# dt goes into the decays' exponent, and the other chunk's values meet their probabilities in three rounded products

## The reference, cut to what matters

```python
dt = softplus(h @ Win.T + dt_bias);  g = dt * A;  G = cumsum(g) within a chunk of 128
x_c     = v * dt[..., None]
decay   = where(causal, exp(G_i - G_j), 0)
y_intra = ((q @ k.T) * decay) @ x_c
k_dec   = k * exp(G_last - G)[..., None]
y_inter = (q * exp(G)) @ state      # state: sum over chunks of k_dec.T @ x_c, decayed
y       = rms_norm(y_intra + y_inter) * gnorm_w * silu(gate);  out = y @ Wo.T
```

## Time and profile before

| what | value |
|---|---|
| median of three executions | 1065.32 us (1064.6 to 1066.32) |
| the profiled execution, its own time | 1066.14 us |
| its span in the profile | 1064.4 us |
| PE busy | 1030.6 us (97%) |
| DVE busy | 785.5 us (74%) |
| ACT busy | 707.6 us (66%) |
| POOL busy | 215.1 us (20%) |
| chain that ended last, by engine | PE 89%, DVE 3%, DMA 3%, issue 2%, ACT 2%, POOL 1% |
| mean granted clock of TensorE | 0.994 |

### The profile page before, as it was taken

The page is one execution under the profiler, slowest core; times in us unless marked ns, Lnnn a source line. Parts: engine busy times, 40 slices in busy tenths (PEclk is TensorE's granted clock), DMA queues, the critical chain, the costliest instruction groups (busy, mean ns, idle before and its releaser), DMA issues.

```text
span 1064.4 us, 14465 instructions
## 1 busy us (share of the span) xinstructions
PE 1030.6 (97%) x4678; PEld 804.4 (76%) x4678; DVE 785.5 (74%) x1543; ACT 707.6 (66%) x1373; POOL 215.1 (20%) x132
## 2 busy tenths in 40 slices
PE   5989999999999999999999999999999798999998
PEld 3767777777777777777777777777777467888786
DVE  6668887887888888878887887888887885334322
ACT  3457877877788788878877877788777655233300
POOL 2212221211222221112121211212223520000000
PEclk8999999999999999999999999999999999999999
DMA  8432411220131013102411220131032303111011
GB/s 312 139 144 65 129 26 40 79 79 20 39 118 39 20 39 118 39 20 65 126 26 39 79 79 20 39 118 39 20 99 60 99 21 128 60 40 60 20 40 40
DMA packets 37947, 74.09 MB, mean 70 GB/s; under 512 B 3264, under 2 KB 19936, under 8 KB 35616
## 3 DMA queue, kind: packets, MB, share of 16 engines
q1 hardware_dynamic: 37056, 73.30, 21.6%
q10 hardware_dynamic: 864, 0.43, 0.1%
HBM read 69.38 MB, written 2.24 MB: 67 GB/s over the span
## 4 chain that ended last, share of the span: by engine, by line
PE 89%; DVE 3%; DMA 3%; issue 2%; ACT 2%; POOL 1%; SPq 0%; DVEq 0%; ACTq 0%; POOLq 0%
PE ps_q_gt L68 14%; PE ps_q_gt L70 14%; PE ps_q_gt L69 14%; PE ps_ss_o L68 5%; PE ps_ss_o L70 5%; PE ps_ss_o L69 5%; PE ps_s_y L798 5%; PE ps_kv_x L70 3%; PE ps_kv_x L69 3%; PE ps_kv_x L68 3%; PE ps_s_y L807 2%; PE ps_kv_x L821 2%; PE ps_s_y L68 2%; PE ps_s_y L69 2%; PE ps_s_y L70 2%
## 5 line engine op out<-in xcount | busy, mean ns | idle before, releaser
L1861 POOL TENSOR_TENSOR q_sin<-q_sin,cst 128x512 f32<-128x512 f32 x64 | 89.5, 1398 | 304.8 <-ACT q_sin L1001 304.8
L1575 DVE SCALAR_TENSOR_TENSOR prob<-ps_s_y,scal,dec 128x128 f32<-128x128 f32 x252 | 70.8, 343 | 76.7 <-PE ps_s_y L798 76.7
L68 PE MATMUL ps_q_gt<-hT_hi,wq_hi 128*128 128x512 f32 x256 | 124.7, 487 | 1.2 <-DVE q_cos L1385 1.2
L1849 POOL TENSOR_TENSOR dec<-dec,future 128x1024 f32<-128x1024 f32 x31 | 74.4, 2401 | 248.6 <-ACT expg L1020 248.6
L68 PE MATMUL ps_ss_o<-wo_hi,z_hi 128*128 128x512 f32 x260 | 103.7, 399 | 1.6 <-DVE z_lo L63 1.6
L68 PE MATMUL ps_q_gt<-hT_hi,wg_hi 128*128 128x512 f32 x256 | 103.6, 405 | 0.0
L70 PE MATMUL ps_ss_o<-wo_hi,z_lo 128*128 128x512 f32 x260 | 102.5, 394 | 0.0
L69 PE MATMUL ps_ss_o<-wo_lo,z_hi 128*128 128x512 f32 x260 | 102.3, 394 | 0.0
L69 PE MATMUL ps_q_gt<-hT_lo,wg_hi 128*128 128x512 f32 x256 | 101.1, 395 | 0.0
L70 PE MATMUL ps_q_gt<-hT_hi,wg_lo 128*128 128x512 f32 x256 | 100.8, 394 | 0.0
L70 PE MATMUL ps_q_gt<-hT_hi,wq_lo 128*128 128x512 f32 x256 | 100.5, 393 | 0.0
(11 more groups left out here) (272 smaller groups left out, 2613.1 us busy)
## 6 DMA issues: line engine op xcount, KB each, us to landing
dec<-gT_dram SPq DMA_DIRECT2D x32, 512.0 KB, 5.6
raw_q<-wq_in SPq DMA_DIRECT2D x32, 256.0 KB, 2.7
raw_g<-wg_in SPq DMA_DIRECT2D x32, 256.0 KB, 2.9
raw_o<-wo_in SPq DMA_DIRECT2D x8, 1024.0 KB, 7.0
raw_pair<-wkv_in SPq DMA_DIRECT2D x8, 512.0 KB, 4.5
raw_pair<-wgu_in SPq DMA_DIRECT2D x7, 512.0 KB, 3.3
raw_gu<-wgu_in SPq DMA_DIRECT2D x6, 512.0 KB, 3.3
x<-x_in SPq DMA_DIRECT2D x2, 1024.0 KB, 9.9
```

Source lines behind the costliest of these rows:

```text
L68: pe.matmul(out, w_hi, x_hi, start=first, stop=False)
L1575: last = nc.vector.scalar_tensor_tensor(prob[:, h], ps_s[:, h * P:(h + 1) * P], scal[:, tile, 1, h:h + 1], dec[:, tile // 2 % 2, h, tile % ...
L1849: nc.gpsimd.tensor_tensor(cells, cells, future[:].unsqueeze(1).broadcast_to([P, GRP * CPB, CHUNK]), ALU.add).then_inc(mask_done, 1)
L1861: nc.gpsimd.tensor_tensor(q2, q2, sinT, ALU.mult).then_inc(qsin_done, 1)
```

## The change

1. **dt moves into the exponent.** dt gets a floor of 1e-20 and stays in `zs2`. ACT takes its logarithm (`zq`), DVE adds that to minus G (`decay_bias`, new), so that exp(dec + scal) holds dt already. `probabilities` is then one TENSOR_TENSOR of 128x512 in place of four SCALAR_TENSOR_TENSOR of 128x128. `tok` and `scal` lose a third of their width.
2. **The other chunk's product is split.** ACT rounds `cross` into `cross_hi` (`split_cross_hi`, new), DVE subtracts into `cross_lo`, which lies over `cross` (`split_cross_lo`, new), and PE does three products with `v_hi` and `v_lo` of the first chunk. This holds for the 30 odd steps of the loop's form; step 5 of the last group (`whole_cross=True`) and step 7 (`y_exact`) keep the whole product.
3. **Copies and places.** The whole copy `v` falls away but for the last group's step 5; `copy_v_whole` is one instruction; `cap` comes before the second splits in even steps; `sel`, `stats` and the gate tiles lie over `cross_hi`.

```diff
-CHAIN_END = CHAIN_DIFF + 1
+CHAIN_END = CHAIN_DIFF + 2
...
-        tok = sb("tok", [P, NT, 3, H])
+        tok = sb("tok", [P, NT, 2, H])
...
-        cross = sb("cross", [P, GRP, CHUNK])
+        cross, cross_hi = sb("cross", [P, GRP, CHUNK]), sb("cross_hi", [P, GRP, CHUNK], F32R)
+        cross_lo = over("cross_lo", [P, GRP, CHUNK], F32R, place["cross"])
...
-            def y_product(g, t):
+            def y_product(g, t, whole_cross=False):
                 b, c = t // 2, t % 2
-                if c == 1:
+                if whole_cross:
                     pe.wait_ge(cross_done, g * 4 + (b + 1))
-                    nc.tensor.matmul(ps_y, v[:, b % 2], cross[:].rearrange("p h i -> p (h i)"),
+                    nc.tensor.matmul(ps_y, v[:], cross[:].rearrange("p h i -> p (h i)"),
                                      start=True, stop=False)
...
                 pe.wait_ge(vlo_done, g * 4 + (b + 1))
+                if c == 1 and not whole_cross:
+                    pe.wait_ge(xlo_done, g * 4 + (b + 1))
+                    three_products(nc.tensor, ps_y, v_hi[:, b % 2, 0], v_lo[:, b % 2, 0], x_hi, x_lo, True, False)
                 pe.wait_ge(phi_done, g * 8 + (t + 1))
...
+            def split_cross_hi(g, b):
+                act.wait_ge(cross_done, g * 4 + (b + 1))
+                nc.scalar.activation(cross_hi[:], cross[:], ACT.Copy).then_inc(xhi_done, 1)
...
+            act.wait_ge(chain, CHAIN_G - 1)
+            nc.scalar.activation(zq, zs2, ACT.Ln).then_inc(exp_done, 1)
             copy_gT(0)
...
+                if c == 0:
+                    split_cross_hi(g, b)
                 round_squares(g, t)
...
+            def decay_bias():
+                dve.wait_ge(chain, CHAIN_DIFF)
+                nc.vector.tensor_tensor(tok[:, :, 0], tok[:, :, 0], zq, ALU.add).then_inc(chain, 1)
...
-                for h in range(GRP):
-                    last = nc.vector.scalar_tensor_tensor(
-                        prob[:, h], ps_s[:, h * P:(h + 1) * P], scal[:, tile, 1, h:h + 1],
-                        dec[:, tile // 2 % 2, h, tile % 2], ALU.mult, ALU.mult)
-                last.then_inc(prob_done, 1)
+                nc.vector.tensor_tensor(prob[:], ps_s.rearrange("p (h i) -> p h i", h=GRP),
+                                        dec[:, tile // 2 % 2, :, tile % 2], ALU.mult).then_inc(prob_done, 1)
...
+            def split_cross_lo(g, b):
+                dve.wait_ge(xhi_done, g * 4 + (b + 1))
+                split_lo(nc.vector, cross_lo[:], cross[:], cross_hi[:]).then_inc(xlo_done, 1)
...
+                if t == 0:
+                    split_cross_lo(g, b)
                 if c == 0:
                     copy_scalars(g, b)
+                if c == 0:
+                    cap(g, t)
                 if t == 0:
                     split_o_lo(g)
-                if c == 0:
-                    cap(g, t)
+                if c == 0 and t > 0:
+                    split_cross_lo(g, b)
                 probabilities(g, t + 1)
```

More of the change, by code:

```diff
@@ L30 @@
 MASKED = -1e30
+DT_FLOOR = 1e-20
 POOL_TILES = 5
@@ L249, in layer @@
         ps_q, ps_g, ps_kv, ps_x, ps_s, ps_y, ps_ss, ps_o = (pair[:, i] for pair in pairs for i in range(2))
-        sel = sb("sel", [P, C_END - C_SEL])
-        gate_mag, gate_T = (sb(n, [P, 2, B, KT]) for n in ("gate_mag", "gate_T"))
+        gate_mag, gate_T = (over(n, [P, 2, B, KT], F32, place["cross_hi"] + i * 8 * B * KT)
+                            for i, n in enumerate(("gate_mag", "gate_T")))
+        sel = over("sel", [P, C_END - C_SEL], F32, place["cross_hi"] + 16 * B * KT)
+        norm_rows = [over("stats", [P, NT, 6], F32, place["cross_hi"] + 16 * B * KT + 64)] + norm_rows
         silu_c = cross[:, 3].rearrange("p (k m) -> p k m", k=KT)
@@ L282, in layer @@
             + [qT[:, 0, i] for i in range(GRP)] + [sg[:, 0, i] for i in range(2)]
-        v_late = over("v_late", [P, D], F32, place["sq_parts"])
+        v_late = over("v_late", [P, CPB, D], F32, place["sq_parts"])
         prob_late = over("prob_late", [P, GRP, CHUNK], F32, place["prob_hi"])
@@ L853, in y_exact @@
                 c = t % 2
-                tile, values = (prob_late, v_late[:]) if c else (prob, v[:, 1])
+                tile, values = (prob_late if c else prob), v_late[:, c]
                 if c == 1:
                     pe.wait_ge(cross_done, KVH * B)
-                    nc.tensor.matmul(ps_y, v[:, 1], cross[:].rearrange("p h i -> p (h i)"),
+                    nc.tensor.matmul(ps_y, v_late[:, 0], cross[:].rearrange("p h i -> p (h i)"),
                                      start=True, stop=False)
@@ L1032, in decays, with copy_v @@
                 last.then_inc(dec_done, 1)
-            def copy_v(g, b):
+            def copy_v(g, b, whole=False):
                 act.wait_ge(kv_ready, g * 4 + (b + 2))
                 ps_v = ps_kv.rearrange("p (c d) -> p c d", c=CPB)[:, :, D:2 * D]
-                nc.scalar.activation(v[:, (b + 1) % 2], ps_v[:, 0], ACT.Copy)
+                if whole:
+                    nc.scalar.activation(v[:], ps_v[:, 0], ACT.Copy)
                 nc.scalar.activation(v_hi[:, (b + 1) % 2], ps_v, ACT.Copy).then_inc(v_done, 1)
+            def split_cross_hi(g, b):
+                act.wait_ge(cross_done, g * 4 + (b + 1))
+                nc.scalar.activation(cross_hi[:], cross[:], ACT.Copy).then_inc(xhi_done, 1)
             def round_squares(g, t):
@@ L1187, in step @@
                     sigmoid(g, t)
-                    copy_v(g, b)
+                    copy_v(g, b, not next_group and t == 2)
                     inverse_rms(g, t)
@@ L1202, in copy_v_whole @@
                 ps_v = ps_kv.rearrange("p (c d) -> p c d", c=CPB)[:, :, D:2 * D]
-                nc.scalar.activation(v[:, (b + 1) % 2], ps_v[:, 0], ACT.Copy)
-                nc.scalar.activation(v_late[:], ps_v[:, 1], ACT.Copy).then_inc(v_done, 1)
+                nc.scalar.activation(v_late[:], ps_v, ACT.Copy).then_inc(v_done, 1)
             def squares_whole(g, t):
@@ L1449, in decay_rates @@
                 nc.vector.scalar_tensor_tensor(zq, zq, 1.0, zs, ALU.add, ALU.mult).then_inc(chain, 1)
-                nc.vector.tensor_scalar(z1, z1, 0.0, None, ALU.max).then_inc(chain, 1)
+                nc.vector.tensor_scalar(z1, z1, DT_FLOOR, None, ALU.max).then_inc(chain, 1)
                 dve.wait_ge(chain, CHAIN_G - 2)
-                nc.vector.scalar_tensor_tensor(tok[:, :, 1], zq, 2.0, z1, ALU.mult, ALU.add)\
+                nc.vector.scalar_tensor_tensor(zs2, zq, 2.0, z1, ALU.mult, ALU.add)\
                     .then_inc(chain, 1)
@@ L1556, in _ @@
             chunk_end()
+            decay_bias()
             cap(0, -2)
```

31 lines of the change are left out of this document (16 added, 15 removed).

## The result

The changed kernel takes 1069.18 us in the median of 15 runs (1066.96 to 1074.81); the kernel before, run beside it, 1065.03 (15 runs, 1062.77 to 1067.86). The ratio is 1.0037, with a 95% interval of 1.0025 to 1.0049: slower by 4.2 us, where 6.1 us less were forecast. The time lies above the range, 1057.3 to 1062.2.

The account below looks back on a forecast made before the run. PE's own queue was taken to bound the loop, other engines the stretch behind it. 4.93 us in the loop plus 1.22 behind it gave 6.15 less than 1065.32, so 1059.2 us, range 1057.3 to 1062.2.

Parts of the forecast that it names:

- as long as before in even steps: Sign of being right, in the loop: PE takes 0.17 us less in odd steps and the same time in even ones.
- The product on PE: Odd loop steps: three products of 0.23 us replace one of 0.86, 0.17 less in 29 steps, 4.93 us.
- The rival that the loop gives nothing: Three short products cost as much as the whole one; only the tail's 1.22 us left, 1064.1; chance 0.05.
- The probabilities on DVE and the lower half of `cross`: DVE in the loop: probabilities at 0.67 us end 0.46 earlier; 30 `cross_lo` of 0.69 fit into idleness, cost nothing.
- the 1.26 named: DVE's cover left ahead of the next tile's scores in the loop: 1.95 us idle less 0.69 for `cross_lo`.
- The rival of POOL's port: POOL's mask holds `cross_lo` in every pair of loop steps, 8.7 us lost in the loop: 1072.8; chance 0.03.
- Behind the loop, 1.22: Shorter probabilities on the path at three places behind the loop, together 1.22 us less.
- the second and third terms: Last group: probabilities of step 4, ahead of the `raw_gu` load, and of step 6 save 0.46 us each.
- The first term: Step 2 of the last group: probabilities release the chain to POOL's mask; about 0.30 of 0.46 us arrives.
- The rival in which the tail gives nothing or takes a hold: Behind the loop: only the loop's gain, 1060.4, or one more hold of 1.4 us, 1061.8; chance 0.26.
- The clock, named as luck: After idle PE the clock fell to half level, costing 1.7 us; the changed kernel may have none or two.
- Before the loop, nothing to 0.6: Logarithm on ACT and added sum on DVE fall into idle time: cost nothing, at worst 0.6 us.

Follow-up runs that it names:

- the kernel before with 64 bytes: Kernel before with an unused tile of 64 bytes a partition ahead of `wq_hi`, no instruction changed: 1073.85 us, ratio 1.0074.
- with 32 bytes: Kernel before with an unused tile of 32 bytes a partition ahead of `wq_hi`, no instruction changed: 1076.16 us, ratio 1.0089.

## Why the prediction was wrong

The step that failed is no term of the sum but what the sum took as fixed: that PE's odd step loses 0.17 and takes "as long as before in even steps". It never asked what the new and smaller tiles do to the places of the others. Durations of the trace of before were carried over to every product that the diff doesn't touch, some 2,400 of them in the loop, and these became 0.233 us apart where they had been 0.229 (gate weights) and 0.232 (`wo`). Moved places alone cost the kernel before 8.2 us (32 and 160) and 10.6 (0 and 128); with either on top, the forecast of 1059.2 would have been 1067.4 or 1069.8, and 1069.18 was measured.

Step by step:

- *The product on PE, 0.17 a step.* Right, and a little small. At the changed kernel's places the three products save 0.18 (11.25 to 11.07), at agreeing ones 0.23; the first makes 30 x 0.18 = 5.4, against 4.93. The rival that the loop gives nothing fell. The three distances stand at 0.23 as forecast:

```profile
320.41 0.39 PE L69 MATMUL ps_s_y<-cross_hi,v_hi 128*128 128x512 f32 x1
320.64 0.39 PE L70 MATMUL ps_s_y<-cross_lo,v_hi 128*128 128x512 f32 x1
320.87 0.40 PE L71 MATMUL ps_s_y<-cross_hi,v_lo 128*128 128x512 f32 x1
321.10 0.40 PE L821 MATMUL ps_s_y<-prob_hi,v_hi 128*128 128x512 f32 x1
```

- *The rest of PE's queue, taken as unchanged.* Wrong. Per pair of steps the changed kernel takes 24.97 and the one with agreeing places 24.61: 0.36 x 30 = 10.8 of the 10.7 us by which the loops differ (751.5 and 740.8). The kernel before was in between, since its weights and scores agreed with the right-hand stack and its `z` did not: at agreeing places its even steps are 13.71, 0.11 less. So the change lost what the kernel before had by luck of its layout (it agreed in part), and a good layout of the changed one gains what that one lacked too.
- *The probabilities on DVE and the lower half of `cross`.* The prices were right, the cover was larger than worked out. The timeline of DVE has, ahead of the odd step's scores:

```profile
315.29 0.69 DVE L64 TENSOR_TENSOR cross_lo<-cross,cross_hi 128x512 fp32r<-128x512 f32 x1
317.82 0.69 DVE L1596 TENSOR_TENSOR prob<-ps_s_y,dec 128x512 f32<-128x512 f32 x1 [1.84 <-PE ps_s_y L803]
```

  1.84 us of idleness in place of the 1.26 named: the queue had already gained the 0.46 of the probabilities before, and `cross_lo` costs 0.60 from start to start in a full queue, not its record's 0.69.
- *The rival of POOL's port.* It fell. 30 records of `cross_lo` take 683 to 689 ns, so none was held, and POOL's mask starts 5.1 us after the start of one:

```profile
320.42 2.40 POOL L1877 TENSOR_TENSOR dec<-dec,future 128x1024 f32<-128x1024 f32 x1 [10.27 <-ACT expg L1028]
```

  The Trainium skill's rule (SBUF — State Buffer, "Who interferes with whom") is neither borne out nor refuted by that, since the two never meet.
- *Behind the loop, 1.22.* Right in kind, and in part by luck of size. The stretch from the scores of step 4 to the first gate and up product, 34.77 to 33.58, gives 1.19, but only the second and third terms lie in it, 0.92; at agreeing places the exponent alone gives 0.80 there, and for the rest no cause was looked for. The first term shows ahead of it: PE's wait for the squares fell by 0.15 for a forecast 0.13. The rival in which the tail gives nothing or takes a hold fell. The load of `raw_gu` is issued 2.20 us behind the scores of step 4, where it was 2.63, for a forecast 0.46:

```profile
829.11 0.48 PE L837 MATMUL ps_ss_o<-sq_parts,ones_r 128*128 128x512 f32 x1 [1.88 <-DVE sq_parts L64]
```

```profile
831.62 0.51 SPq L575 DMA_DIRECT2D raw_gu<-wgu_in  x1
```

- *The clock, named as luck.* One dip more behind the loop than before in the profiled execution, 1.7 us of clock. It belongs to that execution, which is 3.5 us above the median; it does not account for the median.
- *Before the loop, nothing to 0.6.* Can't be told: the start varies by more than that from profile to profile.

Compared at like places the change is faster, as forecast, but not by one number. Where the stacks disagree, the changed kernel takes 1069.2, the kernel before with 64 bytes 1073.85, 4.7 more, and with 32 bytes 1076.16, 7.0 more. The first of these has `wo` and `z` at the pair that costs little, so 7.0 is the better comparison for 6.15. Where all agree at 224, the kernel before takes 1064.35 and the changed one 1054.07, 10.3 less, and here 6.15 was too small: 8.1 of it lies in the loops (748.9 and 740.8), 30 x 0.23 = 6.9 of that in the odd steps' typical length, the rest mostly in PE's waits for the squares, which the changed kernel doesn't have. The sum had priced the loop's gain from DVE at nothing; at agreeing places it isn't.

What stays open: why the left-hand stack 64 bytes below the right-hand one (160 and 224) costs little over a third of what the others do (5.8 of 15.0), and which access of PE the operands' places slow down. A product whose own operands lie both in the left-hand stack, at the same remainder, is slower too when the stacks disagree (those of `cross` with `v`: 0.227 from start to start with both stacks at 160, 0.231 to 0.234 with the right one at 224), so the rule is not one product's own. But with the left at 224 and the right at 192 the second and third of them take 0.227 again, so it does not reach into them at every pair of places. A neighbour's load of the stationary operand beside the product is one candidate; it was not tried. Nor were other agreeing places than 224 and 160.

## What to carry to other kernels

When PE is the bound, look at the addresses of its operands before and after an edit, also one that only shrinks or moves a small tile: a few unused bytes decided over 15 us of 1,054 here, more than the edit itself. Compare two versions at the same remainders, or the layout is measured along with the idea; and before a forecast carries a duration over to untouched instructions, it should say what else they depend on. The hint was in the trace of before: products of `wo` and `z`, whose places disagreed, stood 0.232 apart, and those of `hT` and `wg`, whose places agreed, 0.229, at the same clock.

## What the runs showed of the hardware

- Back-to-back products of rounded 128x512 operands, at a granted clock of 1.00, start 0.227 to 0.228 us apart where the addresses of the two stacks agree by 256 (at 224 and at 160), and 0.232 to 0.233 where they differ, by 32, 64 or 128 bytes, whichever stack was moved; with the left at 160 and the right at 224 they start 0.230 apart. It is so with DVE, ACT and POOL idle too: 0.227 and 0.233.
- Products 256 wide (keys and values, 0.119 to 0.120) and the unrounded scores (0.86) don't show it; but both operands of each lie in the same stack, so this says nothing of the width or of the rounding.
- From the start of the product of `cross` to the last product of the own chunk's probabilities, medians over odd steps at agreeing places, it is 1.33 us with the whole one and 1.13 with the three: 0.20 saved in place of 0.86 - 0.69. Most of the last 0.03 of the step's 0.23 shows in the twelve products of `wo` behind, which take 2.74 us behind the whole product and 2.72 behind the three; why was not looked for.
- Behind idle time of PE the granted clock fell to the half level, at 1.7 us of clock each time, none to twice in the gate and up products of one profile. Whether kernel or chance decides how often, one profile each can't tell. The start of the first scores (74.2 to 78.0) varies too.
